# One bank each for the scores and the turned weights, four banks for the projection steps, and a context's first half turned before the output's turn, in the fourth attention

## The reference

```python
    E = Wq.shape[1]                      # 256, one head
    x1 = layernorm(modality1, ln1_g, ln1_b)       # 100 x 256 of each context
    x2 = layernorm(modality2, ln2_g, ln2_b)       # 361 x 192 of each context
    q = x1 @ Wq + bq
    k = x2 @ Wk + bk
    v = x2 @ Wv + bv
    attn = softmax(q @ k.T * E ** -0.5)           # 100 x 361
    ctx = attn @ v
    return ctx @ Wo + bo
```

## Time and profile before

| | us |
|---|---|
| median of the three runs | 1642.88 |
| the profiled execution, its own time | 1643.71 |
| span of that execution | 1641.5 |
| PE busy, whole kernel | 1502.2 |
| fourth attention, from the first scores to the last output turn | 1390.6 to about 1512 |
| twelve turns, scores of context 2 to scores of context 14 | 91.3 |

### The profile page before, as it was taken

How to read it: one execution, slowest core, us unless ns; L and a number is a source line. 1 busy time by engine, 2 the same in 40 slices (tenths; PEclk the granted TensorE clock), 3 DMA queues, 4 the chain that set the end, 5 groups by cost and what they waited for, 6 DMA issues and landing times.

```text
span 1641.5 us, 30315 instructions
## 1 busy us (share of the span) xinstructions
PE 1502.2 (92%) x9070; PEld 1093.7 (67%) x9070; DVE 899.0 (55%) x2901; ACT 609.0 (37%) x1705; POOL 291.1 (18%) x409
## 2 busy tenths in 40 slices
PE   5999999859999979999999989979999999888886
PEld 2666666659999946777777667748777644565664
DVE  4788787632232225545555435656666455555755
ACT  3655555412233224444444423223444001443422
POOL 4555566330000040000000000110000011121000
PEclk9999999859999999999999989989999799998888
DMA  5111115249999830000000000010110100341000
GB/s 137 31 33 37 36 35 184 85 152 316 323 320 328 293 104 19 19 9 18 18 18 18 0 1 13 20 45 28 36 29 17 33 20 25 91 164 43 1 21 20
DMA packets 89654, 128.85 MB, mean 78 GB/s; under 512 B 17362, under 2 KB 74786, under 8 KB 84450
## 3 DMA queue, kind: packets, MB, share of 16 engines
q1 hardware_dynamic: 85954, 123.50, 23.5%
q0 software_dynamic: 2432, 4.34, 0.9%
q10 hardware_dynamic: 1184, 0.01, 0.0%
HBM read 112.87 MB, written 11.67 MB: 76 GB/s over the span
## 4 chain that ended last, share of the span: by engine, by line
PE 75%; DVE 8%; issue 8%; POOL 3%; ACT 3%; DMA 2%; SPq 0%; POOLq 0%; DVEq 0%; ACTq 0%
PE bank L2353 10%; PE bank L2501 9%; PE bank L2710 8%; PE bank L2361 6%; PE bank L2803 6%; PE bank L2469 5%; PE bank L2520 4%; PE bank L2480 4%; PE bank L2724 4%; PE bank L2756 3%; PE bank L2772 3%; PE bank L2442 2%; PE bank L2956 2%; PE bank L2403 1%; DMA work<-in_F_b1c 1%
## 5 line engine op out<-in xcount | busy, mean ns | idle before, releaser
L1620 DVE COPY work<-bank 128x300 f32<-128x300 f32 (+1 forms) x272 | 124.1, 490 | 143.4 <-PE bank L2480 142.1
L2501 PE MATMUL bank<-work 128*100 128x64 f32 (+1 forms) x1760 | 191.4, 260 | 10.4 <-DVE work L1620 8.6
L2501 PEld LDWEIGHTS bank<-work 128*100 128x100 f32 x1760 | 177.1, 171 | 35.4 <-issue 19.0
L1112 ACT ACTIVATE work<-bank,work 100x361 f32<-100x361 f32 (+1 forms) x272 | 158.9, 590 | 53.2 <-DVE work L1611 37.6
L1955 DVE SCALAR_TENSOR_TENSOR work<-bank,work 128x128 f32<-128x128 f32 x160 | 56.1, 351 | 160.4 <-PE bank L2710 148.4
L2710 PE MATMUL bank<-work 128*128 128x128 f32 x1216 | 142.8, 275 | 0.6 <-DMA work<-in_F_b1c 0.6
L2710 PEld LDWEIGHTS bank<-work 128*128 128x128 f32 x1216 | 140.6, 192 | 2.2 <-ACT work L1233 1.2
L1611 DVE TENSOR_REDUCE work<-bank 100x1 f32<-100x361 f32 x208 | 102.0, 529 | 67.0 <-PE bank L2469 64.5
L2480 PEld LDWEIGHTS bank<-ident,work 100*128 100x128 f32 x880 | 90.6, 143 | 43.7 <-issue 22.5
L2480 PE MATMUL bank<-ident,work 100*128 100x100 f32 x880 | 106.0, 254 | 8.5 <-ACT work L1112 8.1
L1233 ACT ACTIVATE work<-bank,work 128x128 f32<-128x128 f32 x160 | 58.8, 368 | 144.0 <-PE bank L2710 138.9
(11 more groups left out here) (343 smaller groups left out, 2767.0 us busy)
## 6 DMA issues: line engine op xcount, KB each, us to landing
work<-in_F_w SPq DMA_DIRECT2D x58, 1024.0 KB, 5.8
work<-in_ctxT SPq DMA_DIRECT2D x64, 180.5 KB, 2.4
work<-context_norms SPq DMA_DIRECT2D x32, 288.0 KB, 3.4
context_norms<-work SPq DMA_DIRECT2D x16, 288.0 KB
work<-in_ctx SPq DMA_DIRECT2D x16, 192.0 KB, 2.8
work<-in_F_b SPq DMA_DIRECT2D x20, 128.0 KB, 6.8
work<-sorted_x SPq DMA_DIRECT2D x20, 128.0 KB, 3.0
sorted_y<-work SPq DMA_DIRECT2D x20, 128.0 KB, 6.2
```

What stands on the lines that cost most here:

```text
L1112: nc.scalar.activation(pr[:, 0:NK], S_bank[k][0:T, 0:NK], ACT.Exp, bias=nmax[k][0:T, :], accum_out=rsum[j][0:T, h:h + 1]).then_inc(s.exped ...
L1620: nc.vector.tensor_copy(PT[k][:, 0:CH, :], PT_bank[k][:, 0:CH * T].rearrange("p (c t) -> p c t", c=CH)).then_inc(s.probs_copied.sem, 1)
L2501: ins = nc.tensor.matmul(to, PT[k][:, c, :], values, start=(c == 0), stop=(c == CH - 1))
```

## The change

For the fourth attention alone:

- All scores go to bank 0, all turned weights to bank 2. PE's `scores(t)` then waits for `exp(t-1)` instead of `exp(t-2)`, and `probs_turn(t)` for `probs_copy(t-1)` instead of `probs_copy(t-2)`.
- The two banks that come free, 1 and 3, go to the steps: each of the four steps of a context has a bank of its own (6, 7, 1, 3 for steps 0, 1, 2, 3). PE may write step n of context t + 1 as soon as ACT has copied step n of context t.
- PE does step 1 (the context's first half) right behind the scores, ahead of `o_turn(t-1)`; steps 0 and 2 follow behind it. Since PE counts its steps in one semaphore, ACT's copy of step 0 now waits for a count of two steps, as that of step 1 does.

```diff
             if L == 3 and isinstance(t, int) and t == 0:
                 return S_bank[n % 2]
+            if L == 3:
+                return (bank[6], bank[7], bank[1], bank[3])[n]
             return J_bank[(j * STEPS[L] + place_of(L, t, n)) % 2]
...
                         src = step_bank(L, t, j, n)
-                        wait_for(act, s.proj, STEPS[L] * t + place_of(L, t, n) + 1)
+                        wait_for(act, s.proj, STEPS[L] * t + (2 if L == 3 and n < 2 else place_of(L, t, n) + 1))
...
-                    nc.scalar.activation(pr[:, 0:NK], S_bank[k][0:T, 0:NK], ACT.Exp, bias=nmax[k][0:T, :],
+                    nc.scalar.activation(pr[:, 0:NK], S_bank[0 if L == 3 else k][0:T, 0:NK], ACT.Exp, bias=nmax[k][0:T, :],
...
                         dst = step_bank(L, t, j, n)
 
-                        wait_for(pe, s.copied, STEPS[L] * t + place - 1)
+                        if L == 3 and not (isinstance(t, int) and t == 0):
+                            wait_for(pe, s.copied, STEPS[L] * (t - 1) + n + 1)
+                        else:
+                            wait_for(pe, s.copied, STEPS[L] * t + place - 1)
...
                 def scores(t, j, h):
                     n = H * t + h
-                    k = (H * j + h) % 2
+                    k = 0 if L == 3 else h % 2
 
                     if PAIRS[L] == 0:
-                        wait_for(pe, s.exped, n - 1)
+                        wait_for(pe, s.exped, n)
...
                     wait_for(pe, s.exped, n + 1)
-                    wait_for(pe, s.probs_copied, n - 1)
+                    wait_for(pe, s.probs_copied, n if L == 3 else n - 1)
                     for c in range(CH):
-                        ins = nc.tensor.transpose(PT_bank[k][:, c * T:(c + 1) * T], PR[k][0:T, c, :], ident[0:T, 0:T])
+                        ins = nc.tensor.transpose(PT_bank[0 if L == 3 else k][:, c * T:(c + 1) * T], PR[k][0:T, c, :], ident[0:T, 0:T])
...
                 def fourth_attend(t, j, more):
                     started = not (isinstance(t, int) and t == 0)
                     scores(t, j, 0)
+                    if more:
+                        step(t + 1, 1 - j, 1)
                     if started:
                         o_turn(t - 1, 1 - j)
-                    for n in (0, 1, 2):
+                    for n in (0, 2):
                         if more:
                             step(t + 1, 1 - j, n)
```

More of the change, by code:

```diff
@@ L1602, in maximum @@
                             wait_for(dve, s.mask_row, t + 1)
-                        sc = S_bank[k][0:T, 0:NK]
+                        sc = S_bank[0 if L == 3 else k][0:T, 0:NK]
                         apart(dve)
@@ L1610, in maximum @@
                     else:
-                        nc.vector.tensor_reduce(nmax[k][0:T, :], S_bank[k][0:T, 0:NK], axis=AXX, op=ALU.max,
+                        nc.vector.tensor_reduce(nmax[k][0:T, :], S_bank[0 if L == 3 else k][0:T, 0:NK], axis=AXX, op=ALU.max,
                                                 negate=True).then_inc(s.maxed.sem, 1)
@@ L1619, in probs_copy @@
                     wait_for(dve, s.pv, n - 1)
-                    nc.vector.tensor_copy(PT[k][:, 0:CH, :], PT_bank[k][:, 0:CH * T].rearrange("p (c t) -> p c t", c=CH)
+                    nc.vector.tensor_copy(PT[k][:, 0:CH, :], PT_bank[0 if L == 3 else k][:, 0:CH * T].rearrange("p (c t) -> p c t", c=CH)
                                           ).then_inc(s.probs_copied.sem, 1)
@@ L2464, in scores @@
                         for c, m in ((0, CW[0]), (1, CW[1] + 1)):
-                            ins = nc.tensor.matmul(S_bank[k][0:T, 0:NK], QT[j][0:m, c, :], CT[j][0:m, c, 0:NK],
+                            ins = nc.tensor.matmul(S_bank[0 if L == 3 else k][0:T, 0:NK], QT[j][0:m, c, :], CT[j][0:m, c, 0:NK],
                                                    start=(c == 0), stop=(c == 1))
@@ L2468, in scores @@
                         m, b = h // 2, W * (h % 2)
-                        ins = nc.tensor.matmul(S_bank[k][0:T, 0:NK], QT[j][b:b + W, m, :], kt(L, j)[b:b + W, m, 0:NK],
+                        ins = nc.tensor.matmul(S_bank[0 if L == 3 else k][0:T, 0:NK], QT[j][b:b + W, m, :], kt(L, j)[b:b + W, m, 0:NK],
                                                start=True, stop=True)
```

## The result

The changed kernel takes 1626.28 us, the median of four runs (1625.22 to 1626.72), against 1642.23 for the kernel before in the same runs: a ratio of 0.9903, with a 95% interval of 0.9888 to 0.9918. That is 16.0 us less (13.5 to 18.4), where 12.7 was forecast and the range ended at 1627.0. It is faster, as forecast, and by a little more than the range allowed.

What follows compares the result with a forecast made beforehand. A loop through PE, ACT's two copies and DVE's chain was taken to set the fourth attention's 7.36 us turn; 11.2 us from turns plus 1.5 from the clock, 12.7, gave 1630.2 us, range 1627 to 1635.5.

Steps and rivals of the forecast that it cites:

- The second half's bank: Fourth attention's turn: without the second half's wait for ACT's copy, 0.86 us gained a turn, 7.36 to 6.50.
- The first half, hidden by DVE's chain: First half ahead of the output turn: its 0.35 us fit in 0.41 us before DVE's scaling is done, costing nothing.
- The second rival: Output turn comes later by the whole first half: gain 6.6 us, 8.1 with the clock, 1634.8; chance 0.14.
- One bank each: Scores and turned weights with a single bank each: their waits are met long before, so both cost nothing.
- The clock: Two slow turns among the thirteen, 3.1 us over normal: both, one or neither may go; one taken, 1.5 us.
- The first rival: Clock holds throughout the thirteen turns, so both slow stretches go: 11.2 + 3.1 us, 1628.6; chance 0.17.
- The tail: From context 15's scores to the end: no term in the sum, so no change in time was counted.
- The fourth rival: Context's load becomes the bound, holding PE behind the scores: 1651.5 if landings take 7.8 us each; chance 0.04.

Runs made afterwards that it cites:

- Order_only: Kernel before, with only the first half moved ahead of the output turn and the old banks kept: 1644.45 us, ratio 1.0015 to the kernel before.
- banks_only: Kernel before, with only the four step banks and single banks for scores and turned weights, PE's old order: 1627.99 us, ratio 0.9914.
- both_halves_ahead: Changed kernel, with the second half of the next context also ahead of the output turn: 1629.38 us, ratio 0.9908 to the kernel before.
- one_bank_only: Kernel before, with only scores in bank 0 and turned weights in bank 2, steps and order as before: 1641.31 us, ratio 0.9993.
- sooner_and_exp_first: Kernel before with the bank part, DVE's scaling ahead of normalizing x, ACT's exponential ahead of copying x's turn: 1621.43 us, ratio 0.9872.
- after_again: Changed kernel run again unchanged, beside the other experiments: 1627.78 us against 1640.0 for the kernel before, ratio 0.9922.
- later_by_one: Changed kernel with context 0's scores computed twice, delaying all behind them: stage 96.8 us, tail 140.24 us against 138.20.

## Why the prediction was off

Its account of the turn was right. Two terms beside the turn were wrong: the clock's, which was too small, and the rest of the kernel, which was put at nothing without a reason.

*The second half's bank.* The mechanism is right: 6.50 us a turn were forecast, and 78.00 over 12 is 6.50. That the number agrees to 0.01 us is partly luck, for small errors cancel. The forecast took 0.13 us from the exponential to PE, and it is 0.05 (1438.66 less 1438.61). It took 0.54 us from the turned weights to DVE's copy, and it is 0.61 (1439.27 less 1438.66). And the 7.36 us it started from are the mean of four turns of the short kind and three of the long (from the scores of context 7, which the heading of the earlier trace rows calls context 6, to those of context 14); the mean of both kinds is 7.38. So the gain is 0.88 us a turn and not 0.86. Over all contexts 11.2 was forecast and 11.7 measured at full clock (0.23 + 10.6 + 0.88).

*The first half, hidden by DVE's chain.* Right, by 0.06 us of room. Order_only, banks_only and both_halves_ahead show it from three sides: nothing alone, nothing missed without it, 0.15 us a turn (6.65 less 6.50) once the second half is ahead too. The second rival (1634.8) is excluded.

*One bank each.* Nothing, as forecast, by one_bank_only.

*The clock.* This step failed: "So the two slow stretches may go (3.1 us), stay (0), or one goes; I take one, 1.5 us". Both went: none of the ten profiles with four step banks has a half-clock turn in the stage, while the four with two step banks have two, two, two and three. They were worth 2.7 us (8.81 and 8.95 against 7.51, for both are turns of the long kind), not 3.1. The first rival had this, at 0.17. Nothing in the earlier trace rows spoke for one of the two rather than both: that only two of thirteen waits were followed by a fall says how often it falls with the wait there, not how often without it. What brings the clock down stays open. Longer idle pieces did not bring more falls: order_only waits 1.37 to 1.42 us in every turn and has two. Waits of 0.67 and 0.75 us in every turn of both_halves_ahead brought none, and neither did the one wait of 1.28 us in sooner_and_exp_first. The section that the first rival names, "A second HAM failure mode: psum-queue depth-cycling" in "TensorE: Matmul & The Clock Gate" of the Trainium skill, has a kernel whose brief idle pieces between groups of matmuls swing the clock. The trace agrees in this: the waits for a bank went and the swings went with them. It doesn't show why two or three of thirteen waits were followed by one.

*The tail.* This step failed too, and it is the larger: the sum takes 12.7 us off the whole execution, so everything outside the stage was to stay as long as it was, and no reason was given. The profile has 2.6 us there. The layer behind the attention has half-clock stretches of its own, which fall on other instructions from one profile to the next. One such place, in the timelines of the kernel before and then of the changed one, is a product of sixteen matmuls in the slot network, which takes 5.25 us in the one, with a granted clock of 0.51 from 1573.6 to 1577.0, and 3.62 in the other, with a clock of 1.00:

```profile
1573.76 5.25 PE L2956 MATMUL bank<-work 128*128 128x256 f32 x16
```

```profile
1558.36 3.62 PE L2963 MATMUL bank<-work 128*128 128x256 f32 x16
```

Tails of otherwise equal instructions ran from 138.2 to 140.9 us over all kernels here. What the tail does in the timed runs, which have no trace, stays open.

*The sizes.* In the two profiles 17.1 us were gained where 12.7 were forecast. Of the 4.4 between them (4.3 by the rounded parts) the turns have 0.5 (11.7 less 11.2), the clock 1.2 (2.7 less 1.5) and the tail 2.6. In the timed runs the gain was 16.0, and the kernel before was 0.65 us faster beside the changed one (1642.23) than in the runs that the forecast started from (1642.88). The stage alone gives 11.7 + 2.7 = 14.4 us; the two comparisons gave 16.0 and 12.8, on either side of it, with intervals that hold it. With that sum the forecast would have been 1628.5, inside the range. So the clock term alone doesn't explain a result below 1627.0: the range had no room for the rest of the kernel.

*The fourth rival*, late loads: its mechanism exists and is small. In the changed kernel's profile the first half of context 9 came 1.45 us behind context 8's scores instead of 1.22, and since the output turn still waited for DVE until 1.62, that turn took 6.66 us instead of 6.64. About 0.1 had been forecast, for this load. It is late in eight of the ten profiles with four step banks, and lengthens that turn by 0.02 to 0.6 us in seven of them and by 1.2 us in sooner_and_exp_first.

## What to carry to other kernels

When several pieces of work share a buffer in turn, write down for each piece which copy frees it; a wait for a copy of the same item, behind other work of the copying engine, sits in the loop and costs every turn, while a wait for the item before was free here. The second bank of a result that is consumed three microseconds ahead of its next writing was worth nothing here, and such a buffer is the place to take a bank from.

Work moved ahead of an instruction that waits anyway is free only up to the length of that wait, and it becomes a cost as soon as the wait is mended: here the moved half costs 0.16 us a turn once DVE's scaling comes sooner.

The length of a removed wait is not its worth. Of 1.04 us a turn 0.88 were gained, since ACT's exponential was the next limit, and 2.7 us came on top, because the turns at half clock went with the wait. When turns alternate, take the mean over as many of either kind. And a few us of difference in a stretch whose code didn't change should be tested with a delay before any cause is given to it.

## What the runs showed of the hardware that was not expected

A delay of 1.2 us ahead of the stage's end made the tail 2.0 us longer on top. PE's busy time in it rose from 112.84 to 114.14 us, with the same matmuls, while DVE's and ACT's busy times stayed within about 0.1 us. With a delay of 2.6 us it was 139.0, so the effect does not grow with the delay.

The mean granted clock doesn't tell how long the tail is: it was 0.87 in banks_only, 0.85 in the changed kernel and 0.84 in after_again, with tails of 138.3, 138.2 and 138.2 us, and 0.84 in later_by_one too, with 140.2.

The kernel before had two half-clock turns in one profile and three in another, with the same instructions and the same idle microsecond in each turn.
